# Both ends of the attention in a fused GRU, attention and gated-FFN kernel are rebuilt: preparation moved into the recurrence's last steps, the end reordered, weights rounded by ScalarE

## The reference

```python
# 1. GRU over time on x (W_ih, W_hh: 256 x 768), start = cond -> h_t for 32 steps
r = sigmoid(i_r + h_r); z = sigmoid(i_z + h_z); n = tanh(i_n + r * h_n); h = (1 - z) * n + z * h
# 2. attention over the GRU's states, with 4 heads of 64; x + attention
x = x + softmax(q k^T / 2) v @ Wo + bo
# 3. a second recurrence, driven by that x: four Runge-Kutta stages per step
dq = q - q**3 / 3 - p + drive + tanh(q) @ coupling.T + bias;  dp = EPSILON * (q + ALPHA - BETA * p)
# 4. gated FFN on its states, weights rounded to -1, 0, 1 times a scale, activations to int8; x + FFN
weight_quant(w) = clip(round(w / mean|w|), -1, 1) * mean|w|      # three matrices, 256 x 832
silu(bitlinear(y, w_gate)) * bitlinear(y, w_up) -> bitlinear(., w_down)
```

## Time and profile before

| what | value |
|---|---|
| time, median of 3 runs | 663.62 us (660.6, 663.62, 669.09) |
| profiled execution, device time | 668.23 us |
| its span | 666.1 us |
| busy: TensorE, VectorE, ScalarE, GpSimd | 597.2, 542.3, 396.9, 263.5 us |
| mean granted clock of TensorE | 0.97 of full speed |

### The profile page before, as it was taken

How to read it: one execution, slowest core, us unless ns; L and a number is a source line. 1 busy time by engine, 2 the same in 40 slices (tenths; PEclk the granted TensorE clock), 3 DMA queues, 4 the chain that set the end, 5 groups by cost and what they waited for, 6 DMA issues and landing times.

```text
span 666.1 us, 13898 instructions
## 1 busy us (share of the span) xinstructions
PE 597.2 (90%) x4842; PEld 524.3 (79%) x4842; DVE 542.3 (81%) x1543; ACT 396.9 (60%) x962; POOL 263.5 (40%) x406
## 2 busy tenths in 40 slices
PE   8899999999996769997578999999999999999984
PEld 7899999999996668885466777777777777777762
DVE  3667767777766887897779999999999999999971
ACT  3554454454542434762246787878878787787764
POOL 0323323323321724312434455554545545555521
PEclk9999999999999999998779999999999999999996
DMA  8300000000000002100000000000000000000000
GB/s 288 116 3 1 1 2 1 1 2 1 1 1 17 1 1 106 66 1 1 1 0 1 9 18 10 17 17 17 10 17 17 9 17 17 17 10 17 17 18 24
DMA packets 11972, 14.85 MB, mean 22 GB/s; under 512 B 1600, under 2 KB 9344, under 8 KB 11904
## 3 DMA queue, kind: packets, MB, share of 16 engines
q1 hardware_dynamic: 11904, 13.97, 6.2%
HBM read 9.78 MB, written 4.19 MB: 21 GB/s over the span
## 4 chain that ended last, share of the span: by engine, by line
PE 65%; DVE 24%; ACT 4%; issue 4%; DMA 1%; SPq 1%; ACTq 0%; POOLq 0%; DVEq 0%
PE PS L414 21%; PE PS L306 16%; PE PS L324 12%; PE PS L470 5%; PE PS L485 3%; DVE q_s L923 3%; DVE h_s L913 2%; PE PS L392 2%; DVE h_s L1006 2%; DVE big L786 2%; PE PS L370 2%; DVE PS L881 2%; DVE q_s L937 2%; DVE PS L913 1%; ACT big L556 1%
## 5 line engine op out<-in xcount | busy, mean ns | idle before, releaser
L414 PE MATMUL PS<-h_s 128*128 128x128 f32 x1408 | 191.0, 285 | 15.1 <-DVE PS L881 7.0
L414 PEld LDWEIGHTS PS<-h_s 128*128 128x128 f32 x1408 | 171.2, 195 | 27.4 <-DVE PS L886 10.8
L306 PE MATMUL PS<-part 128*128 128x256 f32 x924 | 119.9, 287 | 3.0 <-DVE part L737 3.0
L306 PEld LDWEIGHTS PS<-part 128*128 128x128 f32 x924 | 113.8, 193 | 3.2 <-issue 3.2
L608 ACT ACTIVATE h_s<-h_s 128x128 f32<-128x128 f32 x256 | 69.0, 304 | 75.6 <-DVE h_s L913 48.1
L324 PE MATMUL PS<-big,wrk 128*128 128x128 f32 x744 | 88.4, 275 | 4.6 <-DVE big L733 4.6
L324 PEld LDWEIGHTS PS<-big,wrk 128*128 128x128 f32 x744 | 85.8, 192 | 5.2 <-DVE big L733 5.2
L1025 POOL COPY h_s<-big 128x256 f32<-128x256 f32 x32 | 21.2, 662 | 135.0 <-DVE big L733 135.0
L913 DVE SCALAR_TENSOR_TENSOR h_s<-PS,h_s 128x128 f32<-128x128 f32 x192 | 50.2, 288 | 12.2 <-PE PS L414 5.5
L907 DVE SCALAR_TENSOR_TENSOR h_s<-PS,h_s 128x256 f32<-128x256 f32 x128 | 53.2, 416 | 0.4 <-ACT PS L609 0.2
L529 ACT ACTIVATE big<-big 128x256 f32<-128x256 f32 x32 | 13.3, 416 | 65.4 <-DVE big L712 65.4
(11 more groups left out here) (140 smaller groups left out, 1209.8 us busy)
## 6 DMA issues: line engine op xcount, KB each, us to landing
out<-q_s SPq DMA_DIRECT2D x32, 128.0 KB, 1.7
x_s<-in_xT SPq DMA_DIRECT2D x14, 256.0 KB, 6.6
k_s<-in_wgT SPq DMA_DIRECT2D x1, 832.0 KB, 6.0
k_s<-in_wuT SPq DMA_DIRECT2D x1, 832.0 KB, 7.6
k_s<-in_wih SPq DMA_DIRECT2D x3, 256.0 KB, 4.8
wrk<-in_whh SPq DMA_DIRECT2D x1, 768.0 KB, 6.9
h_s<-in_wdT SPq DMA_DIRECT2D x1, 768.0 KB, 6.4
x_s<-in_xT SPq DMA_DIRECT2D x4, 128.0 KB, 3.5
```

The source lines that it names most:

```text
L306: r = pe.matmul(p, y, x, start=i == 0, stop=i == len(passes) - 1)
L414: return pe.matmul(PS[:, m, 0:128], w, x, start=False, stop=True, skip_group_check=True)
```

## The change

- **First recurrence.** In step 30 VectorE also makes wv_hi, before the step's work, and in step 31 wv_lo. qk_out of steps 30 and 31 goes from ahead of L729 to behind L733; in step 31 one output ahead of the low half and one behind it.
- **Last four units.** All passes with the state's high half first, 16 matmuls, which wait for ScalarE's s_hi alone; then the 8 with the low half. VectorE takes out the first two units, ScalarE the other two (s_qka). Ahead of these ScalarE runs an exp on one column, which loads the table, and makes v_hi[0].
- **Begin of attention.** GpSimd's zero fill starts after the last low half and h_s, no longer after all qk outputs; ScalarE makes wo_hi in step 0, VectorE wo_lo in step 1.
- **Features.** They lie per half kk in a bank, keep_feats and the projection go half by half, and the last step's have banks 3 and 4 of their own. project(5, 1) and (7, 1) go to bank 2.
- **FFN weights.** Rounding is now ScalarE adding a large constant (weight_round, in steps 5 and 6 ahead of exp, and in step 0 of the second recurrence), then two VectorE passes (weight_top, weight_quant) instead of two comparisons and a difference. GpSimd has no part in it.
- **End of attention.** residual(5, .) leaves step 7 and comes behind the loop, then start values, constants and the up matrix, keep_feats(7), residual(6, .), the first cubic, residual(7, .). ScalarE's first tanh and square run before the drive, and the drive's first block is made in 128 and 384 columns.

The diff, cut to its core:

```diff
...
-        feats = PS[:, 5:7, :].rearrange("p g n -> p (g n)").rearrange("p (g k n) -> p g k n", g=4, k=2)
+        feats = [PS[:, 5:7, :]] * 7 + [PS[:, 3:5, :]]
...
-        out_bank = lambda i, m: {(6, 1): 0, (7, 0): 1, (7, 1): 3}.get((i, m), 7)
+        out_bank = lambda i, m: {(5, 1): 2, (6, 1): 0, (7, 0): 1, (7, 1): 2}.get((i, m), 7)
...
+        drive_done = lambda t: 2 * (t // 4) + 4 if t else 2
...
-                    pe.wait_ge(s_hlo, min(2 * a + 2, T - 1))
-                    if a == 15:
-                        pe.wait_ge(s_hlo31, 1)
+                    pe.wait_ge(s_hlo, 2 * a + 2)
...
+            pe.wait_ge(s_hi, T)
             for u in last:
-                bulk_unit(u)
+                w, m = divmod(u[2], 2)
+                ms = slice(m * 128, (m + 1) * 128)
+                slot_free(pe, u)
+                for k in range(2):
+                    for y in (wqk_lo, wqk_hi):
+                        pe.matmul(bulk_bank(u), raw(y[:, w, k, ms]), raw(h_hi[1][:, k, :]), start=k == 0 and y is wqk_lo,
+                                  stop=False)
+            pe.wait_ge(s_hlo, T - 1)
+            pe.wait_ge(s_hlo31, 1)
+            for u in last:
+                w, m = divmod(u[2], 2)
+                for k in range(2):
+                    r = pe.matmul(bulk_bank(u), raw(wqk_hi[:, w, k, m * 128:(m + 1) * 128]), raw(h_lo[1][:, k, :]),
+                                  start=False, stop=k == 1)
+                r.then_inc(s_bulk, 1)
...
-                    pe.wait_ge(s_qk, 64)
+                    pe.wait_ge(s_qk, 62)
+                    pe.wait_ge(s_qka, 2)
...
-                if i:
-                    pe.wait_ge(s_F, i)
+                if i == 7:
+                    pe.wait_ge(s_sc, 8)
+                elif i:
+                    pe.wait_ge(s_F, 2 * i)
...
+                elif (i, m) == (6, 0):
+                    pe.wait_ge(s_add, 11)
+                elif (i, m) == (7, 1):
+                    pe.wait_ge(s_add, 12)
...
-                pe.wait_ge(s_F, i + 1)
-                passes = [(w[:, k, ms], x[:, k, :]) for k in range(2)
-                          for w, x in ((wo_lo, f_hi[i]), (wo_hi, f_lo[i]), (wo_hi, f_hi[i]))]
-                for n, (w, x) in enumerate(passes):
-                    r = pe.matmul(PS[:, bank, :], raw(w), raw(x), start=n == 0, stop=n == 5)
+                for k in range(2):
+                    pe.wait_ge(s_F, 2 * i + k + 1)
+                    passes = [(w[:, k, ms], x[:, k, :]) for w, x in ((wo_lo, f_hi[i]), (wo_hi, f_lo[i]), (wo_hi, f_hi[i]))]
+                    for n, (w, x) in enumerate(passes):
+                        r = pe.matmul(PS[:, bank, :], raw(w), raw(x), start=k == 0 and n == 0, stop=k == 1 and n == 2)
...
+            ac.wait_ge(s_const, 1)
+            ac.activation(wsum[:, 3:4], ones[:, 0:1], ACT.Exp)
+            ac.wait_ge(s_hb, T)
+            ac.activation(raw(v_hi[0]), h_s[:, :, 0:512], ACT.Copy).then_inc(s_vs0, 1)
+            for u in last[2:]:
+                kind, j, i = u
+                dst = k_s[:, i % 2, :].rearrange("p (b t) -> p t b", t=T)[:, 2 * j:2 * j + 2, :]
+                ac.wait_ge(s_bulk, number[u] + 1)
+                ac.activation(dst, bulk_bank(u).rearrange("p (t b) -> p t b", t=2), ACT.Identity,
+                              bias=ba[:, 1, i % 2:i % 2 + 1]).then_inc(s_qka, 1)
...
+            def weight_round(w):
+                if w == 0:
+                    ac.wait_ge(s_mag, 1)
+                ac.wait_ge(s_wrec, w + 1)
+                ac.activation(w_src[w], w_src[w], ACT.Identity, scale=wscale[:, w:w + 1],
+                              bias=mag[:, 0:1]).then_inc(s_wrnd, 1)
...
+                    if i in (5, 6):
+                        weight_round(i - 5)
...
+                    if i == 0:
+                        ac.wait_ge(ld_wo, 16)
+                        ac.activation(raw(wo_hi), wo_s, ACT.Copy).then_inc(s_wo, 1)
...
+                if slot == 0:
+                    ac.wait_ge(s_F, 16)
...
-            ac.wait_ge(s_cb, 1)
-            ac.wait_ge(s_add, 16)
-            for k in range(2):
-                drive_block(0, k)
...
+                if t == 0:
+                    weight_round(2)
+                    ac.wait_ge(s_cb, 1)
+                    ac.wait_ge(s_add, 16)
+                    for k in range(2):
+                        drive_block(0, k, 0, 128)
+                    for k in range(2):
+                        drive_block(0, k, 128, 512)
...
+                if t == T - 2:
+                    ve.wait_ge(ld_wv, 16)
+                    ve.wait_ge(s_bulk, number["gi", 15, 5] + 1)
+                    ve.tensor_copy(raw(wv_hi), wv_s[:, :, :]).then_inc(s_wv, 1)
+                if t == T - 1:
+                    ve.wait_ge(s_wv, 1)
+                    ve.tensor_tensor(raw(wv_lo), wv_s[:, :, :], wv_hi, ALU.subtract).then_inc(s_wv, 1)
...
-                if n == 15:
-                    for u in qks:
-                        qk_out(u)
...
-                if t == T - 1:
+                if t < T - 1:
+                    for u in qks:
+                        qk_out(u)
+                else:
                     hi, lo = (a[1][:, :, B:2 * B] for a in (h_hi, h_lo))
+                    qk_out(qks[0])
                     ve.wait_ge(s_hi, T)
                     ve.tensor_tensor(raw(lo), hn, hi, ALU.subtract).then_inc(s_hlo31, 1)
-                if n < 15:
-                    for u in qks:
-                        qk_out(u)
+                    qk_out(qks[1])
...
-            for u in last:
+            for u in last[:2]:
                 qk_out(u)
-
-            ve.wait_ge(ld_wv, 16)
-            ve.wait_ge(s_bulk, number[last[-1]] + 1)
-            ve.tensor_copy(raw(wv_hi), wv_s[:, :, :]).then_inc(s_wv, 1)
-            ve.wait_ge(s_wv, 1)
-            ve.tensor_tensor(raw(wv_lo), wv_s[:, :, :], wv_hi, ALU.subtract).then_inc(s_wv, 1)
-            ve.wait_ge(s_hb, T)
-            ve.tensor_copy(raw(v_hi[0]), h_s[:, :, 0:512]).then_inc(s_vs0, 1)
...
-            ve.wait_ge(ld_wo, 16)
-            ve.tensor_copy(raw(wo_hi), wo_s).then_inc(s_wo, 1)
-            ve.wait_ge(s_wo, 1)
-            ve.tensor_tensor(raw(wo_lo), wo_s, wo_hi, ALU.subtract).then_inc(s_wo, 1)
...
-                ve.wait_ge(s_wrec, w + 1)
-                ve.tensor_scalar(w_dst[w], w_src[w], wscale[:, w:w + 1], 0.5, ALU.mult, ALU.is_gt).then_inc(s_wup, 1)
-
-            def weight_lower(w):
-                ve.wait_ge(s_wup, w + 1)
-                ve.tensor_scalar(w_src[w], w_src[w], wscale[:, w:w + 1], -0.5, ALU.mult, ALU.is_lt).then_inc(s_wlow, 1)
-
-            def weight_half(at):
-                ve.wait_ge(s_wlow, 3)
-                ve.tensor_tensor(w_dst[2][:, at:at + 896], w_dst[2][:, at:at + 896], w_src[2][:, at:at + 896],
-                                 ALU.subtract).then_inc(s_wd, 1)
...
+            def weight_top(w):
+                ve.wait_ge(s_wrnd, w + 1)
+                ve.tensor_scalar(w_dst[w], w_src[w], MAGIC, 1.0, ALU.subtract, ALU.min).then_inc(s_wtop, 1)
+
+            def weight_quant(w):
+                ve.wait_ge(s_wtop, w + 1)
+                ve.tensor_scalar(w_dst[w], w_dst[w], -1.0, None, ALU.max).then_inc(s_wd if w == 2 else s_wq, 1)
+
+            def start_values():
+                condf = flat(cond[:, :, :])
+                ve.wait_ge(s_split, 7)
+                ve.wait_ge(s_S, 8)
+                ve.tensor_copy(qn[0], condf)
+                ve.tensor_scalar(pn[0], condf, SH, U, ALU.subtract, ALU.mult).then_inc(s_q0, 1)
+                ve.wait_ge(ld_cb, 16)
+                ve.tensor_scalar(cb[:, :], cb[:, :], SH, U, ALU.subtract, ALU.mult).then_inc(s_cb, 1)
...
+            for i in range(8):
+                if i >= 5:
                     weight_mean(i - 5)
-                if i < 8:
-                    maximum(i)
-                if i >= 2:
+                    weight_scale(i - 5)
+                maximum(i)
+                if i == 1:
+                    ve.wait_ge(s_wo, 1)
+                    ve.tensor_tensor(raw(wo_lo), wo_s, wo_hi, ALU.subtract).then_inc(s_wo, 1)
+                if 2 <= i < 7:
                     residual(i - 2, 0)
...
+                if i == 6:
+                    weight_top(0)
+                    weight_quant(0)
+            residual(5, 0)
+            residual(5, 1)
+            start_values()
+            weight_top(1)
+            weight_quant(1)
+            keep_feats(7)
+            residual(6, 0)
+            residual(6, 1)
...
+            cubic(0, qn[0])
+            residual(7, 0)
+            residual(7, 1)
...
-            po_.wait_ge(s_qk, 64)
+            po_.wait_ge(s_hlo31, 1)
+            po_.wait_ge(s_hlo, T - 1)
...
+                    if i == 0:
+                        po_.wait_ge(s_bulk, number[last[-1]] + 1)
...
-                if i == 6:
-                    po_.wait_ge(s_wlow, 1)
-                    po_.tensor_tensor(w_dst[0], w_dst[0], w_src[0], ALU.subtract).then_inc(s_wq, 1)
...
```

(43 more changed lines are left out.)

60 lines of the change are left out of this document (18 added, 42 removed).

## The result

The changed kernel takes 646.9 us (median of four runs, 645.4 to 649.8), the one before 663.99 beside it: ratio 0.972, interval 0.967 to 0.976. It is faster by 17.1 us. On another chip a second series gave 651.1 against 667.1, ratio 0.976 (0.971 to 0.981). Forecast: 643 us, 636 to 652.

What follows compares the result with a forecast made beforehand. VectorE bounds the second recurrence, TensorE steady attention, an engine-to-engine chain attention's begin. Gains 11.0 + 8.0 + 3.0 + 0.7 = 22.7, 20.7 after one lost race: 647.5 us profiled, 643 us as median, range 636 to 652.

Steps and rivals of the forecast that it cites:

- the five distances of the table: Stretches between trace marks from step 30 to the third seed; forecast gains 0.95, 2.45, 7.6, 8.0 and 3.7 us.
- one lost race: Three L777 in attention steps 1, 2, 5 race GpSimd's L1046; one expected lost, costing about 2 us.
- Outputs behind the state: First recurrence, steps 30 and 31: qk_out behind the new state saves 0.95 us twice, less 0.2; gain 1.7.
- Last projections: Before attention: 24 matmuls start earlier and run at full clock in 3.0 us; scores 3.4 earlier, outputs' gain included.
- Locks of the first softmaxes: Attention steps 0 and 1: L769 and L777 no longer held by GpSimd's L1046; gains 1.5, 1.4 and 1.6 us.
- the 3.98 us pause: Before the first output projection: starting on its first half gains 0.5 us, full clock afterwards 1.3.
- The race of step 5: Attention step 5: L777 starts ahead of GpSimd's L1046 by 0.1 us; a loss would cost about 2 us.
- The end, 8.0: End of attention: TensorE starts step 0 of the second recurrence at 318.05 instead of 326.04, 8.0 us earlier.
- Steps 0 and 1, 3.7: Second recurrence: step 0 gains 3.0 us by fewer weight passes and full clock, the next step 0.7.
- more is lost: Rival: two or three lost races and one or two more half-clock stretches; gain 12 to 17, 647 to 652 us; chance 0.20.
- one end doesn't shorten: Rival: another input holds the second recurrence's begin, 8.0 and 3.0 go, 652 us remain; gain 5 to 12; chance 0.10.
- the slower rival: Second recurrence: the 30 later steps don't settle at 9.8 us, each losing 1.4; 685 us; chance 0.03.

Runs made afterwards that it cites:

- the outputs ahead: The changed kernel with qk_out of steps 30 and 31 put back ahead of L729's product; one run, 648.7 us.
- the late zero fill: The changed kernel with GpSimd's zero fill again waiting for the last q and k outputs; one run, 649.0 us.
- the end alone: The changed kernel with the begin's edits put back and the end's edits kept; 0.978 of the kernel before the change, 14.5 us less.
- all splits held: The changed kernel, every GpSimd split but the first waiting for VectorE's normal of the step before; 648.0 us, 0.969 of the kernel before the change.
- holds and fills: The changed kernel with every GpSimd split but the first held back and idle matmuls in three TensorE pauses; 644.6 us (0.966), in another series 643.1 us.
- the unchanged kernel: The changed kernel itself, without any follow-up edit, not the kernel before the change; 646.9 us (0.972), on another chip 651.1 us (0.976).

## Why the forecast was right, and where not

Time and direction were right: 643 forecast, 646.9 measured, inside 636 to 652. Part of that is luck. The sum had 22.7 us in the five distances of the table, 20.7 after one lost race; they gave 15.6 in this profile, and 2.8 more came from outside the change. The same luck flatters the absolute marks: scores at 216.51 (216 to 217 forecast), L810 at 221.75 (221.7) and L818 at 224.14 (224.1) match only because step 30 began 1.98 earlier. Counted from step 30, each came about 2 us later than forecast, and the first seed, 309.97 (306 to 308), about 4 to 6. By its steps:

- **Outputs behind the state, gain 1.7.** 0.95 in step 31's begin as counted, and 1.4 up to the end of L784, the new state of step 31 (from the start of step 30's matmuls 11.26 instead of 12.68). The 0.3 that is missing is the wv_lo subtraction, priced at about 0.6 by L769. It took 0.94, and the first gate instruction behind it starts 1.75 us after step 31's matmuls instead of 1.26, a loss of 0.49 where 0.2 was counted.

```profile
205.23 0.94 DVE L763 TENSOR_TENSOR part<-wv_s,part 128x512 fp32r<-128x512 f32 x1
```

- **Last projections, 1.7 more.** The order works (16 matmuls start on the high half), but the step "2.04 was followed by full clock and 3.05 by half, so I take full clock" failed. The pause was 2.02 us and half clock followed: the 24 matmuls took 4.6 us, 1.6 of the 2.2 that are missing in this stretch; they also started 0.3 late, and the scores followed 0.25 later behind them than counted. The length of the last pause alone doesn't decide: 2.04 was followed by full clock before, by half with the outputs ahead; 2.02 by half here, 2.03 by full with the late zero fill; 3.05 by half before, 3.04 by full with the end alone. With this pause filled the stretch took 10.7 us in all three profiles, 1.5 less. What sets the clock apart from the length of the pause stays open.
- **Locks of the first softmaxes, and the 3.98 us pause.** Right to 0.3: 7.85 against 7.6. L818 of step 0 came first by 0.41 (forecast 0.3), and steps 1 and 2 were won by 0.16 and 0.28 (0.25 and 0.15).
- **The race of step 5.** The margin of 0.1 was lost, as I half expected. ScalarE's pass took 1.77, not 1.58. The Abs pass that I priced it by has no operand per partition for scale and bias; that this is the reason was not tried. What failed is the price of a lost race, "about 2 us": the distance behind it grew by 3.3 (3.2 for step 4), and with all splits held 2.9 came back up to the second recurrence. Normal's delay of 2.2 goes on to the mean, for which TensorE waited 2.08 instead of 0.25, and the half clock behind that wait adds 1.5.

```profile
267.93 1.77 ACT L610 ACTIVATE k_s<-k_s,mag,wscale 128x1664 f32<-128x1664 f32 x1
```

- **The race of step 4** I had not listed: its margin was 0.26 before. In every kernel with the new begin exp of step 4 starts 0.28 us later after the maximum than before (1.06 instead of 0.78), which leaves nothing. The kernel with the end alone keeps the 0.78 and the margin of 0.26. Why exp is later with the new begin stays open; nothing in the changed instructions of that step explains it, and it was not tried.
- **weight_quant.** 0.59 us for the gate matrix (0.68 and 0.62 for the other two), between the ends 0.5 and 1.1, nearer to the lower. My 0.8 was too much; the estimate from the Trainium skill (VectorE: DVE Perf Modes, the perf-mode tier table), 0.56, was closer.
- **The end, 8.0.** Right as a sum: 7.5 where no race is lost. With the race it was 4.6.
- **Steps 0 and 1, 3.7.** Step 0 took 13.65 us in the first profile, longer than the 13.17 before: the half clock stayed. "The half clock of 326 to 332 should be gone, as the pause before it is about 2 us" failed in the same way as above. In the profiles at full clock both steps gain 5.8, which is more than I had counted, and in this one 1.9.
- **The rivals.** What happened lies between the forecast and "more is lost": one race, three stretches at half clock, and a gain of 17.1, at the border of the two. In "one end doesn't shorten" the 652 us leave out the race that the forecast holds; 643 and the missing 11.0 make 654. The loop settled at a median of 9.75 us per step in every kernel; the slower rival never showed.

With holds and fills the five distances add up to 23.8 us, where 22.7 was counted without a lost race. In short, with both disturbances taken out the begin gave 10.6 of the 11.0 forecast and the end 7.5 of 8.0; steps 0 and 1 gave 5.7 instead of 3.7. Most of the error was in two things: which of two instructions starts first, VectorE's or GpSimd's, and TensorE's clock. The single edits of the end (features by halves, rounding on ScalarE, the new order) were not tried one by one, so its 7.5 is shown only as a sum.

## What to carry to other kernels

When an edit moves a VectorE operation with two SBUF inputs to within a few tenths of a GpSimd operation that reads SBUF, don't trust the margin: let the one off the path wait for the other by a semaphore. In a row of such races hold all: with one held, another was lost in the same profile, and with all held none was, in four profiles of three kernels. Where TensorE must pause ahead of a dense chain, try idle matmuls in the pause: here no cost was seen, and between profiles that ran at half clock and those with the fill lie 4.1 us at the begin of the second recurrence and 1.5 in the last projections. Four and six runs of the kernel with holds and fills lie within 1.7 and 2.6 us, the unchanged kernel's within 4.4 and 5.1. And before a forecast by absolute marks is called right, measure from a mark ahead of the change.

## What was not expected of the hardware

Half clock is not fixed by the length of the pause ahead: behind the same 2.08 us step 0 of the second recurrence ran at 1.2 GHz in both profiles of the changed kernel and at 2.4 GHz in four of its variants, none of which changed anything within 10 us ahead of it. The changed kernel's mean clock went from 0.973 to 0.987 over eight runs on two chips, with 8.4 us between the ends; with the pauses filled it was 0.982 to 0.994 in 20 runs of three kernels. The lock between VectorE and GpSimd held for the rest of GpSimd's instruction: in the losses with rows for both here (2.85, 2.90, 2.35, 2.21, 2.71 us) VectorE ended 0.55 to 0.56 us behind GpSimd's instruction, whenever it had started.
